# Block sums and normalised rows in PSUM, work moved from GpSimd to the scalar and vector engines, two jobs moved later

## What is computed

```python
def reference(x, adj, W):              # x (8, 2048, 128), adj (2048, 2048), W (128, 128)
    h = maximum(layernorm(x), 0)       # over the last axis, eps 1e-5
    A = relu((adj + adj.T) * 0.5)
    d = sum(A, axis=1) ** -0.5         # 0 where the sum is 0
    L = eye(2048) - d[:, None] * A * d[None, :]
    out = einsum('nm,bmo->bno', L, h @ W)
    return x + relu(out)
```

## Time and profile before

| | us |
|---|---|
| median of 3 runs | 437.81 |
| the runs | 436.41 to 440.29 |
| the profiled execution | 435.52 |
| its span, first to last instruction | 433.7 |
| busy: tensor, vector, scalar, GpSimd | 379.2, 309.9, 178.1, 185.0 |

### The profile page before, as it was taken

How to read it: one execution, slowest core, us unless ns; L and a number is a source line. 1 busy time by engine, 2 the same in 40 slices (tenths; PEclk the granted TensorE clock), 3 DMA queues, 4 the chain that set the end, 5 groups by cost and what they waited for, 6 DMA issues and landing times.

```text
span 433.7 us, 6127 instructions
## 1 busy us (share of the span) xinstructions
PE 379.2 (87%) x2097; PEld 198.4 (46%) x2097; DVE 309.9 (71%) x696; ACT 178.1 (41%) x379; POOL 185.0 (43%) x247
## 2 busy tenths in 40 slices
PE   3528778987799999997999994999999999999993
PEld 3528753433244444434454542544444444444441
DVE  2787999978579999899887685138845972885142
ACT  1555977554267678758844112102301320132010
POOL 0197702078976566475520551241415252432102
PEclk9877999999999999998999997999999999999998
DMA  8999994101244414332434027940131023103203
GB/s 272 354 371 385 383 273 125 26 0 59 65 121 131 124 39 130 104 97 82 149 119 147 0 73 249 348 143 13 49 97 51 0 74 90 30 26 97 74 0 97
DMA packets 72990, 54.98 MB, mean 127 GB/s; under 512 B 3200, under 2 KB 64768, under 8 KB 72960
## 3 DMA queue, kind: packets, MB, share of 16 engines
q1 hardware_dynamic: 72960, 54.60, 39.9%
HBM read 39.91 MB, written 14.68 MB: 126 GB/s over the span
## 4 chain that ended last, share of the span: by engine, by line
DVE 25%; issue 24%; POOL 17%; DMA 14%; PE 9%; SPq 5%; ACT 5%; POOLq 0%; DVEq 0%; ACTq 0%
DMA out_dram<-sums 7%; POOL form L540 5%; DMA sums<-in_x_dram 4%; POOL hbuf L497 4%; POOL sums L519 4%; DVE form L823 3%; DVE S L768 3%; SPq L363 3%; DMA S<-in_adj_dram 2%; DVE stats L728 2%; PE ps L1087 2%; PE ps L1088 2%; PE ps L1089 2%; DVE S L749 2%; DVE form L815 1%
## 5 line engine op out<-in xcount | busy, mean ns | idle before, releaser
L1087 PE MATMUL ps<-S,hbuf 128*128 128x512 f16 x240 | 91.5, 381 | 6.9 <-DVE S L768 6.9
L1088 PE MATMUL ps<-S,hbuf 128*128 128x512 f16 x256 | 97.5, 381 | 0.0
L519 POOL TENSOR_TENSOR sums<-res,sums 128x512 f32<-128x512 f32 x32 | 46.8, 1462 | 117.1 <-DVE res L885 106.3
L1089 PE MATMUL ps<-S,hbuf 128*128 128x512 f16 x240 | 91.2, 380 | 0.0
L1099 PE MATMUL ps<-S,hbuf 128*128 128x512 f16 x160 | 61.3, 383 | 0.0
L1100 PE MATMUL ps<-S,hbuf 128*128 128x512 f16 x160 | 61.2, 382 | 0.0
L1101 PE MATMUL ps<-S,hbuf 128*128 128x512 f16 x160 | 61.1, 382 | 0.0
L540 POOL TENSOR_TENSOR form<-hbuf 128x1024 f32<-128x1024 f16 x16 | 35.1, 2205 | 31.8 <-DVE S L835 16.9
L664 ACT ACTIVATE g<-ps 128x512 f16<-128x512 f32 x32 | 18.5, 589 | 72.7 <-DVE ps L860 24.4
L621 ACT ACTIVATE S<-S,dneg 128x512 f16<-128x512 f32 x54 | 37.7, 714 | 18.9 <-DVE S L768 17.0
L1037 PE MATMUL ps<-ident,S 128*128 128x128 f32 x160 | 24.4, 318 | 20.1 <-issue 12.0
(11 more groups left out here) (117 smaller groups left out, 688.1 us busy)
## 6 DMA issues: line engine op xcount, KB each, us to landing
S<-in_adj_dram SPq DMA_DIRECT2D x16, 1024.0 KB, 12.1
hbuf<-in_x_dram SPq DMA_DIRECT2D x64, 128.0 KB, 3.4
sums<-in_x_dram SPq DMA_DIRECT2D x32, 256.0 KB, 2.8
out_dram<-sums SPq DMA_DIRECT2D x32, 256.0 KB, 2.3
t_forms<-form SPq DMA_DIRECT2D x48, 128.0 KB, 1.8
S<-t_forms SPq DMA_DIRECT2D x5, 1024.0 KB, 9.5
S<-t_forms SPq DMA_DIRECT2D x1, 768.0 KB, 10.7
S<-t_forms SPq DMA_DIRECT2D x1, 256.0 KB, 8.8
```

The source lines that it names most:

```text
L519: nc.gpsimd.tensor_tensor(sums[:, e % SUMS, :], res[:, e % 2, :], sums[:, e % SUMS, :], ALU.add).then_inc(sum_ready, 1)
L1087: nc.tensor.matmul(acc, h_hi, l_hi(t), start=(mt == 0), stop=False)
L1088: nc.tensor.matmul(acc, h_hi, l_lo(t), start=False, stop=False)
L1089: last = nc.tensor.matmul(acc, h_lo, l_hi(t), start=False, stop=(mt == T - 1))
```

## The change

- **T tiles in PSUM.** The form buffer is gone. `form_t` computes T1, T2, T4 one after the other, in place, in PSUM bank 4; `split_t_hi` and `split_t_lo` read it there. The float16 halves go to four slots of the SBUF buffer work, and one DMA spills both. `split_t_hi(n)` waits for the spill of n - 4. The plain tiles have banks 0 to 3 (`PLAIN_ACCS`).
- **Normalised x in PSUM.** From unit 8 (before: 16) on, scalar normalises, into bank 5. Vector makes all low halves (`split_h_lo`). GpSimd keeps L497 for units 0 to 7 and the short steps. `statistics` of units from 12 on waits for the GpSimd instructions that read mv (`ln_v_ready`). Units 8 to 15 are split in slots 13 to 31.
- **Pairs.** Vector joins, into one buffer for pairs instead of two. Quarter 0 has two pairs in slots 114 and 119, the others in its parts 0 and 1. Every later quarter has two in parts 4 and 5 of the quarter before and two in its own parts 0 and 1.
- **Later rows.** In the parts `finish_product` on vector scales in PSUM, then takes relu and adds x in one instruction. GpSimd does no `add_x` there.
- **Later in time.** T3 is split in the parts 0 to 3 of quarter 0, two pieces in each. The diagonals of row tiles 8 to 15 are taken with the forms. The products with W move to slots 7 and 10 of the next stage, and in the parts by three to nine steps. At the end, `sum_c21` and `split_g_lo` come before the last two tiles are finished.
- **Buffers.** Three sums buffers instead of two; `p1_v`, `w_u` in work instead of S and xn.

The core of the diff:

```diff
-W_AT = (5, 7)
-ADD_AT = (8, 10)
-STORE_AT = (11, 13)
+W_AT = (7, 10)
+ADD_AT = (9, 12)
+STORE_AT = (11, 14)
+FIRST_W_AT = (3, 6)
+FORM_AT = (1, 3, 5)
-PAIR_AT = (4, 5, 6)
+PAIR_AT = (4, 5)
-W_PART_AT = ((3, 1), (6, 0), (6, 7))
+W_PART_AT = ((4, 3), (6, 3), (7, 4), (8, 4))
-SUMS = 2
+SUMS = 3
+PLAIN_ACCS = 4
...
-    h_slot += [16, 18, 20, 22, 24, 26, 28, 30]
+    h_slot += [13, 15, 18, 20, 23, 25, 28, 31]
...
-    first_pair_slot = [T * (PLAIN - 1) + 3 * p for p in range(UNITS // 2)]
+    first_pair_slot = [T * (PLAIN - 1) + 2, T * (PLAIN - 1) + 7]
...
-            return x_buf(u, b0, b1) if u < 2 * UNITS else xn[:, u % XN, b0 * P:b1 * P]
+            return x_buf(u, b0, b1) if u < UNITS else ps[:, XN_BANK, b0 * P:b1 * P]
...
+        def w_at(r, i):
+
+            q, k = r // len(ORDER), r % len(ORDER)
+            if r == 0 and i in FIRST_W_AT:
+                return [PLAIN_TILES - 2 + FIRST_W_AT.index(i)]
+            if r == PARTS - 1 and i == HALF - 1:
+                return [TILES - 2]
+            tiles = [PLAIN_TILES + 4 * q + W_PART_AT.index((k, i))] if (k, i) in W_PART_AT else []
+            if q and (k + len(ORDER), i) in W_PART_AT:
+                tiles.append(PLAIN_TILES + 4 * (q - 1) + W_PART_AT.index((k + len(ORDER), i)))
+            return tiles
...
-                sp.dma_start(t_forms[n % 3, 0, n // 3], form16[:, (n - 1) % FORM_SLOTS, WIDE:2 * WIDE]).then_inc(t_out[n % 3], 16)
-                sp.dma_start(t_forms[n % 3, 1, n // 3], form16[:, n % FORM_SLOTS, 0:WIDE]).then_inc(t_out[n % 3], 16)
+                sp.dma_start(t_forms[n % 3, n // 3], form16[:, n % FORM_SLOTS, :]).then_inc(t_out[n % FORM_SLOTS], 16)
...
+                act.wait_ge(t_ready, n + 1)
+                if n >= FORM_SLOTS:
+
+                    act.wait_ge(t_out[n % FORM_SLOTS], 16 * (n // FORM_SLOTS))
+                nc.scalar.activation(form16[:, n % FORM_SLOTS, 0:WIDE], ps[:, T_BANK, :], ACT.Copy).then_inc(t_hi_ready, 1)
...
-                if u >= 2 * UNITS + LN_SLOTS:
-                    dve.wait_ge(rstd_ready, (u - LN_SLOTS - 2 * UNITS) // LN_BATCH + 1)
+                if u >= UNITS + LN_SLOTS:
+                    dve.wait_ge(ln_v_ready, 2 * ((u - LN_SLOTS - UNITS) // LN_BATCH + 1))
...
+            def form_t(n):
+
+                i, f = n // 3, n % 3
+                t = ps[:, T_BANK, :]
+                if n:
+                    dve.wait_ge(t_lo_ready, n)
+                if f == 0:
+                    dve.wait_ge(b12_ready, i + 1)
+                    nc.vector.scalar_tensor_tensor(t, s_piece(chain_of("B11", i)), npos[:, i:i + 1],
+                                                   s_piece(chain_of("T3", i)), ALU.mult, ALU.add).then_inc(t_ready, 1)
+                else:
+                    mt = i + HALF
+                    nc.vector.scalar_tensor_tensor(t, s_piece(chain_of(["B22", "B21"][f - 1], i)), dneg[:, mt:mt + 1], t,
+                                                   ALU.mult, ALU.subtract).then_inc(t_ready, 1)
...
             def combine_pair(n):
 
-                dve.wait_ge(pair_ready, n + 1)
-                a11, a21, a12, a22 = (pair_buf(n)[:, :, i * P:(i + 1) * P] for i in range(4))
+                q, p = n // (UNITS // 2), n % (UNITS // 2)
+                u = q * UNITS + 2 * p
+                dve.wait_ge(h_lo_ready, UNITS * QUARTERS)
+                if n:
+
+                    dve.wait_ge(s_lo_ready, n)
+                else:
+                    wait_spilled(dve)
+                nc.vector.tensor_tensor(pair_buf, hbuf[:, u:u + 2, 0, :], hbuf[:, u:u + 2, 1, :], ALU.add).then_inc(s_chain, 1)
...
+            def finish_product(e):
+                dve.wait_ge(prod_done, e + 1)
+                slot, count = dsv_slot(e)
+                dve.wait_ge(dsv_ready, count)
+                dve.wait_ge(sum_ready, e)
+                dve.wait_ge(sums_in[e % SUMS], 16 * (e // SUMS + 1))
+                prod = ps[:, 6 + e % 2, :]
+                nc.vector.tensor_tensor(prod, prod, dsv[:, slot, :], ALU.mult).then_inc(prod_scaled, 1)
+                dve.wait_ge(prod_scaled, e - PLAIN_TILES + 1)
+                nc.vector.scalar_tensor_tensor(sums[:, e % SUMS, :], prod, 0.0, sums[:, e % SUMS, :], ALU.max,
+                                               ALU.add).then_inc(sum_ready, 1)
...
-                if tau < T - LEAD - 1:
+                if tau < HALF - LEAD - 1:
                     take_diag(tau + LEAD + 1)
...
+                if r < HALF // 2:
+                    for i in range(2):
+                        split_l_lo(T3_FROM + 2 * r + i)
                 for c in taken_in(r):
-                    take_product(c)
+                    if c < PLAIN_TILES:
+                        take_product(c)
+                    else:
+                        finish_product(c)
...
-            take_product(TILES - 2)
             sum_c21(QUARTERS - 1)
             split_g_lo(TILES - 1)
-            take_product(TILES - 1)
+            finish_product(TILES - 2)
+            finish_product(TILES - 1)
```

More of the change, by code:

```diff
@@ L70, in gnn_layer @@
     PIECES = G * T
+    T3_FROM = PIECES - HALF
     ORDER = [1, 2, 6, 3, 5, 7, 4]
@@ L132, in gnn_layer @@
         dsv = sb("dsv", [P, 2, WIDE])
-        form = sb("form", [P, FORM_SLOTS, WIDE])
-        form16 = form[:].bitcast(F16)
+        work = sb("work", [P, FORM_SLOTS, WIDE])
+        form16 = work[:].bitcast(F16)
         ident = sb("ident", [P, P])
@@ L149, in gnn_layer, with summed @@
         w_sum, w_sb = (res[:, 1, i * P:(i + 1) * P] for i in range(2))
-        deg = xn[:, 0, 0:4 * T].rearrange("p (i t) -> p i t", i=4)
-        deg_part = form[:, 0, 0:T * G].rearrange("p (t c) -> p t c", t=T)
+        deg = work[:, 3, 0:4 * T].rearrange("p (i t) -> p i t", i=4)
+        deg_part = work[:, 0, 0:T * G].rearrange("p (t c) -> p t c", t=T)
         ps = ctx.enter_context(nc.psum_tensor("ps", [P, 8, WIDE], F32))
-        p1_v = S[:, HALF - 1:T:HALF, 7 * WIDE // 2:4 * WIDE]
-        w_16 = xn[:, 0, :].rearrange("p (a c) -> p a c", a=2)
-        def two(q, k):
-            return ps[:, part_bank(q, k), :].rearrange("p (a c) -> p a c", a=2)
-        def pair_buf(n):
-            return form[:, n % 2 * 2:n % 2 * 2 + 2, :]
+        p1_v, w_u = (work[:, i, :] for i in (2, 3))
+        pair_buf = work[:, 0:2, :]
+        def summed(q, k):
+            return ps[:, part_bank(q, k), :]
+        T_BANK, XN_BANK = 4, 5
         def x_buf(u, b0=0, b1=GRP):
@@ L490, in normalise @@
                 pool.wait_ge(ln_chain, at + LN_OPS)
-                if first >= 2 * UNITS:
+                if not early:
                     nc.gpsimd.tensor_tensor(neg_mean, neg_mean, y, ALU.mult).then_inc(rstd_ready, 1)
@@ L549, in _ @@
                     add_x(PAIR * (s - 1) + ADD_AT.index(tau % T))
[L550 to L567 removed]
+            scale_rows(2)
+            add_x(PLAIN_TILES - 2)
+            add_x(PLAIN_TILES - 1)
+            scale_rows(3)
         @block.scalar
@@ L656, in copy_p1 @@
                 else:
-                    act.wait_ge(l_lo_ready, PIECES)
-                nc.scalar.activation(p1_v, two(q, 1), ACT.Copy).then_inc(p1_copied, 1)
+                    wait_spilled(act)
+                nc.scalar.activation(p1_v, summed(q, 1), ACT.Copy).then_inc(p1_copied, 1)
             def split_g_hi(e):
@@ L841, in sum_c11 @@
                 dve.wait_ge(part_done, part_at(q, 2) + 1)
-                nc.vector.tensor_tensor(two(q, 2), two(q, 2), p1_v, ALU.add).then_inc(c11_ready, 1)
+                nc.vector.tensor_tensor(summed(q, 2), summed(q, 2), p1_v, ALU.add).then_inc(c11_ready, 1)
             def sum_w(q):
@@ L849, in sum_w @@
                     dve.wait_ge(c21_ready, q)
-                else:
-                    dve.wait_ge(h_lo2_ready, 2 * UNITS)
-                nc.vector.tensor_tensor(w_16, two(q, 6), p1_v, ALU.add).then_inc(w_ready, 1)
+                nc.vector.tensor_tensor(w_u, summed(q, 6), p1_v, ALU.add).then_inc(w_ready, 1)
             def sum_c12(q):
@@ L871, in sum_c21 @@
                 dve.wait_ge(u_ready, q + 1)
-                nc.vector.tensor_tensor(two(q, 4), two(q, 4), w_16, ALU.add).then_inc(c21_ready, 1)
+                nc.vector.tensor_tensor(summed(q, 4), summed(q, 4), w_u, ALU.add).then_inc(c21_ready, 1)
             def split_g_lo(e):
@@ L985, in _ @@
                             split_t_lo(3 * i + f)
-                    for r in range(4):
+                    for f in range(3):
+                        if form_slot[i] + FORM_AT[f] == tau:
+                            if i == 0 and f == 0:
+                                dve.wait_ge(d_ready, 3)
+                            if f == 0:
+                                take_diag(HALF + i)
+                                dve.wait_ge(s_diag, HALF + i + 1)
+                            form_t(3 * i + f)
+                            if f == 0:
+                                third_form(i)
+                    for r in range(3):
                         if form_slot[i] + CHAIN_LO[r] == tau:
```

(14 more changed lines are left out.)

217 lines of the change are left out of this document (75 added, 142 removed).

## The result

| | before | after |
|---|---|---|
| median, us | 437.88 (4 runs, 436.41 to 440.29) | 409.95 (4 runs, 409.15 to 410.6) |
| ratio | 1 | 0.9356, interval 0.931 to 0.9403 |
| the profiled execution, us | 435.52 | 410.6 |
| its span, us | 433.7 | 408.8 |
| busy: tensor, vector, scalar, GpSimd | 379.2, 309.9, 178.1, 185.0 | 376.0, 318.8, 189.1, 81.0 |

The account below looks back on a forecast made before the run. Tensor engine bound, with 26.7 us of stalls that all end with the vector engine. Stalls down to 3.0 (23.7 gained) and 1.65 of tail take the span from 433.7 to 408.3, execution 410.1; 411 forecast, range 405 to 421.

Parts of the forecast that it names:

- (a): Stages 0 and 1, to 115: tensor engine waits for `split_l_lo`; 8.3 us of stall, 1.3 to be left.
- (b): Plain stages 2 to 6: three waits for `split_g_lo`, 5.7 us, plus 1.6 of lower clock; 1 to be left.
- (c): Handover from plain stages to parts: 5.57 us idle, then slow matmuls; 8.5 us of stall, all to go.
- (d): Later parts: six waits of the tensor engine, 2.5 us of stall, 0.7 to be left.
- rival B: Vector becomes the bound of the plain stages: 6.4 us there, 3 in stages 0 and 1, 420 us; chance 0.17.
- D: Slower: scalar's normalise and vector's h_lo alternate on one bank, 33 us a stage, 452 us; chance 0.04.
- step (2): Plain stages 2 to 6: vector needs 23.8 us a stage, its lag reaches 10.1 against 9.8 of room.
- (1): Stages 0 and 1: vector's 6.7 us wait for GpSimd goes; of 8.3 us of stall 1.3 stay.
- step (3): Pairs at the handover: join on vector 1.2 us, the 8.5 us go, pair 3 fits by 1.2, no stall.
- X: End of the last plain stage, from which the handover is timed; pair 3 wanted 15.6 us after it.
- Rival C: Third part waits for pair 3 or the reload, with lower clock behind: 415 to 417 us; chance 0.12.
- step (5): Tail: 1.25 us from an earlier L872, 0.8 from the last product, 0.4 lost to product 30: 1.65 gained.

Follow-up runs that it names:

- f0: The changed kernel itself, unaltered, run again beside the e and f kernels; 408.78 us, ratio 0.9307.
- f3: Changed kernel with products with W, their adds and stores back in their old slots; 413.53 us, ratio 0.9414.
- f2: Changed kernel plus idle GpSimd work, three short 128x128 products for each of units 16 to 31; 410.24 us, ratio 0.933.
- g1: Changed kernel plus idle GpSimd work, one long 128x512 product for each of units 16 to 31, and two sums buffers; 413.86 us, ratio 0.9456.
- f1: Changed kernel with the join of the pairs back on GpSimd; 409.74 us, ratio 0.9329.
- g2: Changed kernel with `take_product` on vector and `add_x` on GpSimd back in the parts; 409.02 us, ratio 0.9342.
- e4: Kernel before with eight mv slots, later products with W, and two of quarter 0's four pairs moved into parts 0 and 1; 430.77 us, ratio 0.9835.
- e3: Kernel before with LN_SLOTS 8 instead of 4 and the products with W of the plain stages later; 437.98 us, ratio 0.9996.
- g3: Changed kernel with the first idle matmuls of the front reordered, 17 straight behind the last adjacency transposition; 408.76 us, ratio 0.9332.
- e1: Kernel before with LN_SLOTS 8 instead of 4, more slots for mv; 434.9 us, ratio 0.9924.
- e2: Kernel before with only the products with W of the plain stages later; 438.54 us, ratio 1.0011.

## Why the prediction was right, and where its sizes were off

**The stalls.** Right in all four places: (a) 8.3 to 0.9, forecast 1.3; (b) 7.3 to nothing, forecast 1; (c) 8.5 to nothing, forecast 0; (d) 2.5 to nothing, forecast 0.7. Sum 1.0 against 3.0. The tests it named came out: no L728 waiting for L497; 2.2 us for `split_l_lo`, 0.2 over the 2 that was set (1.6 of it the start, so 0.6 within the work); nothing for `split_g_lo` before the last tile, and none of them later than 9.3 us into its stage; parts from 245.05; a join of 1.216 against 1.2; `split_h_lo` waiting 11.5 us, under the 20 that would have spoken for rivals B and D. Span 408.8 against 408.3.

**Errors cancelled in that span, by luck.** The stalls were 2.0 less than forecast and the tail 0.4 more; the front was 2.1 longer for a reason outside the change. 408.3 - 2.0 + 0.4 + 2.1 = 408.8. Without the accident of the front the span is f0's 406.6.

**Profiled execution and median.** The prediction added 1 us because the median of before lay 2.3 above the profiled execution. That execution turned out to be an unusually quick one (435.52, where the longer series of before have medians of 438.1 to 440.1); the first of after was the slowest of its four. So the spans differ by 24.9 and the medians by 27.9. Of the 3 us between, 2.4 lie between before's profiled execution and its median, in executions that have no profile, and 0.6 between after's median and its first execution, the profiled one.

**The lag in the plain stages, step (2).** The mechanism held, its course did not. Forecast: 5 us at stage 2, then 1.7 more a stage, 10.1 in stage 5, room 9.8. In f0, from the stages' starts to `split_g_lo`: 6.0, 5.8, 5.4 and 9.3 in stages 2 to 5, then 4.2 and 0.2. From stage 2 to stage 5 vector took 23.1 us a stage (forecast 23.8, tensor engine 22.06), but all of the growth came in one stage, 25.9 us, against 21.8 and 21.7. The peak was right to 0.8 by luck, as a mean over unequal stages. Half a microsecond of room was left, not none: f3, with 7.2 of room, f2, with 0.8 us more lag, and g1, with 3.8 more, all fell over this edge, in this stage. That makes rival B, with 0.17, fairly priced rather than generous: 16 GpSimd instructions bring its 6.4 us in the plain stages about, though not its 3 in (1).

The forecast took the 25.8 us of vector between two `split_g_lo` for what would fall. It did not fall: the same stretch, 162.23 to 188.15 in the changed kernel, is 25.9 us, with vector busy for 23.4 of it in both. The stretched instructions are nearly gone, but four `split_h_lo` (2.7 us, new to vector there) and 2.4 us of waiting for scalar's normalise stand in their place. What changed is the rest: vector enters this stretch 5.4 us late instead of 7.0, and the product behind it is wanted 2.6 us later. The lag stops at 9.3 instead of 10.7 for a room of 9.8 instead of 7.2.

**GpSimd's company.** The prediction took L815's and L800's long instructions for contention and put 1 us a stage on what would be left. Right as to the cause (g1) and high as to the rest: in f0 two instructions of stages 2 to 6 are stretched, by 0.5 and 0.9 us. What it had not seen is that the price hangs on the length of GpSimd's instruction (f2 against g1).

**PSUM in place of SBUF.** The prediction went by the row, not by the Trainium skill (VectorE: DVE Perf Modes, "The TRN2 errata"), by whose fixed cycles the estimate is 65 ns more for each. The trace has the same instruction in one line with either source: L726 with a median of 691 ns from PSUM and 682 from SBUF. The measurement decides, and the 0.9 us a stage that the prediction worked out from the rule would have used up the room that was left. Scalar's normalise went the other way, 447 ns in the median into PSUM against 478 into SBUF.

**The handover, step (3).** The reload was not late. Pair 3 came at X + 15.5 (X = 245.05, last split to 260.6), forecast X + 14.4, wanted X + 15.6: the margin was 0.1 and not 1.2, since the last split was stretched from 1.29 to 3.06 us by GpSimd's two adds. f1 went past it, by 0.35. Rival C was nearer than its 0.12 suggests, though at this price it costs tenths of a microsecond.

**The tail, step (5).** 1.25 for a forecast of 1.65. The earlier L872 (L845 now) gave 1.3, as forecast. The term that failed is the last product: 0.8 saved by two vector instructions in place of one and GpSimd's 1.26, less 0.4 for product 30 in between. From the last `split_g_lo` to the end of the last add it is 3.66 us before (427.31 to 430.97) and 3.65 after (402.41 to 406.06), so the net gain over the old order is nothing; over the new order with GpSimd's adds (g2) it is 0.2.

**What each part is worth** was settled for four: later products 4.7 (f3), joins on vector 0.5 of stall (f1), adds on vector 0.2 (g2), all within the changed kernel; and idle work like GpSimd's old long instructions, 4.4 (g1). T in PSUM and normalisation by scalar were not undone one by one, since their buffers hang together, so their shares are not shown. Both act only in the plain stages. There e4 has 8.9 of its 22.2 us of stall left and the changed kernel 0.9, so with the moved diagonals they can be worth about 8. The other 13 us of e4 lie in the parts, 10.4 of them behind the chain of joins and adds. The traces speak for a share of theirs in (b): `split_g_lo` is 12.6 and 12.8 us late in stage 5 of e3 and e4 and 9.3 in the changed kernel, and the wait for a spill, 2.1 and 2.6 us, is gone. Of (d), e4 keeps two stalls of 0.6 us in later parts; they went with an edit that was not tested alone.

None of the variants is shown to beat the changed kernel; g3 may, by 0.7 us at the medians.

## What to carry to other kernels

When one engine feeds another through several places in a row, a fix at one place hands the time to the next: e1, e2 and e3 gave 3, 0 and 0 us, e4 gave 7, and only the whole change gave 28. Before crediting an engine with a long wait, read its program order: in e4 a join of 2 us stood before a gap of 8, because it came behind an add that waited for a DMA. And slack in slots (when a product is wanted) is worth the lag that it covers at the worst stage, with the low clock that follows a wait on top (2.5 us of waiting and 1.7 of clock in f3), so look at the worst stage, not at the mean.
